# Other waiting times in the list scheduler that orders a transformer block's instructions

## The reference

```
x = x + layernorm(attention(layernorm(x)))
x = x + layernorm(ffn(layernorm(x)))
attention: qkv = x @ Wqkv.T + b;  16 query heads, 8 key heads of 128, in pairs
           p = softmax(q1 k1) - lam * softmax(q2 k2)   (causal)
           o = rmsnorm(p @ v) * w;  out = o @ out_w.T + b
ffn:       Hadamard transform, silu(gate) * up (1024 wide), Hadamard, down
```

## Time and profile before

| | |
|---|---|
| median of 3 runs | 1295.7 us (1291.06 to 1301.3) |
| profiled execution | 1293.1 us, span 1291.3 us |
| PE busy | 1168.3 us, 90% |
| DVE busy | 1064.9 us, 82% |
| ACT busy | 1025.2 us, 79% |
| POOL busy | 852.8 us, 66% |
| mean granted TensorE clock | 0.987 |

### The profile page before, as it was taken

How to read it: one execution, slowest core, us unless ns; L and a number is a source line. 1 busy time by engine, 2 the same in 40 slices (tenths; PEclk the granted TensorE clock), 3 DMA queues, 4 the chain that set the end, 5 groups by cost and what they waited for, 6 DMA issues and landing times.

```text
span 1291.3 us, 26698 instructions
## 1 busy us (share of the span) xinstructions
PE 1168.3 (90%) x8110; PEld 829.5 (64%) x8110; DVE 1064.9 (82%) x2723; ACT 1025.2 (79%) x2596; POOL 852.8 (66%) x1208
## 2 busy tenths in 40 slices
PE   6888999889899989899899898999888888889998
PEld 4556766566676666566666666567665565677887
DVE  5888999898979998988889988888788998946545
ACT  4778898798878889898889889897878888856341
POOL 3387777665676676666667776656659896776532
PEclk8999999999999999999999999999999999999999
DMA  3054545554355445444554555534564454640001
GB/s 127 26 106 81 99 87 86 86 102 82 48 121 96 88 85 93 97 76 76 103 97 81 95 84 86 102 68 90 103 97 87 75 106 88 101 93 1 29 17 37
DMA packets 368156, 106.64 MB, mean 83 GB/s; under 512 B 359312, under 2 KB 365712, under 8 KB 367504
## 3 DMA queue, kind: packets, MB, share of 16 engines
q1 hardware_dynamic: 366672, 103.37, 43.8%
q10 hardware_dynamic: 1344, 1.57, 0.4%
HBM read 14.71 MB, written 2.10 MB: 13 GB/s over the span
## 4 chain that ended last, share of the span: by engine, by line
PE 44%; DVE 30%; issue 8%; POOL 6%; ACT 6%; DMA 5%; SPq 2%; ACTq 0%; DVEq 0%; POOLq 0%
DVE p L1473 7%; DVE mx L1459 6%; PE score_bank L1187 6%; PE score_bank L1052 5%; PE score_bank L1058 4%; PE score_bank L1055 4%; DVE score_bank L1454 3%; ACT e_all L1227 3%; DVE negmx L1466 3%; POOL e_all L1748 2%; DMA oT<-o 2%; PE turn_bank L1080 2%; PE turn_bank L1082 2%; PE turn_bank L1081 2%; DMA p16T<-p 2%
## 5 line engine op out<-in xcount | busy, mean ns | idle before, releaser
L1227 ACT ACTIVATE e_all<-score_bank,negmx,few 128x512 f32<-128x512 f32 (+2 forms) x576 | 413.1, 727 | 64.1 <-DVE negmx L1466 50.9
L1748 POOL TENSOR_TENSOR e_all<-e_all 128x512 f32<-128x512 f32 (+3 forms) x320 | 367.8, 1164 | 36.4 <-ACT e_all L1242 24.1
L1052 PE MATMUL score_bank<-k,q 128*128 128x512 f16 (+2 forms) x640 | 223.8, 350 | 53.5 <-issue 24.9
L1459 DVE TENSOR_REDUCE mx<-score_bank 128x1 f32<-128x512 f32 (+1 forms) x384 | 241.4, 636 | 28.0 <-PE score_bank L1058 27.1
L1473 DVE SCALAR_TENSOR_TENSOR p<-e_all,gain,p 128x512 f16<-128x512 f32 (+3 forms) x320 | 248.1, 791 | 6.6 <-ACT p L1249 6.1
L1055 PE MATMUL score_bank<-k,q 128*128 128x512 f16 (+2 forms) x640 | 223.0, 348 | 0.3 <-DVE k L1534 0.3
L1058 PE MATMUL score_bank<-k,q 128*128 128x512 f16 (+2 forms) x640 | 223.0, 348 | 0.0
L1249 ACT ACTIVATE p<-e_all,gain 128x512 f16<-128x512 f32 (+3 forms) x320 | 203.1, 665 | 22.2 <-POOL e_all L1748 21.8
L1799 POOL TENSOR_SCALAR ratio<-s,inv,neg_lam 128x1 f32<-128x1 f32 x128 | 57.1, 446 | 168.4 <-DVE inv L1736 168.0
L1052 PEld LDWEIGHTS score_bank<-k,q 128*128 128x128 f16 x640 | 62.2, 97 | 138.0 <-issue 60.2
L1080 PE MATMUL turn_bank<-v,p16T 128*128 128x256 f16 x512 | 140.5, 274 | 9.4 <-DMA p16T<-p 9.3
(11 more groups left out here) (377 smaller groups left out, 2779.0 us busy)
## 6 DMA issues: line engine op xcount, KB each, us to landing
p16T<-p SPq DMA_TRANSPOSE x320, 3.1
w_raw<-in_w_qkv_dram SPq DMA_DIRECT2D x3, 1024.0 KB, 5.7
w_raw<-in_w_o_dram SPq DMA_DIRECT2D x4, 512.0 KB, 3.4
oT<-o SPq DMA_TRANSPOSE x128, 2.5
bv<-in_hidden_dram SPq DMA_DIRECT2D x8, 256.0 KB, 2.9
w_raw<-in_w_ug_dram SPq DMA_DIRECT2D x4, 512.0 KB, 3.5
out_dram<-e SPq DMA_DIRECT2D x16, 128.0 KB, 1.7
e<-in_w_d_dram SPq DMA_DIRECT2D x1, 1024.0 KB, 6.8
```

What stands on the lines that cost most here:

```text
L1052: pe.matmul(bank[:, 0:w], qh, kh, start=True, stop=False)
L1227: act.activation(e, S[k % NS][:, 0:w], ACT.Exp, bias=negmx[:, d % 2, m, s:s + 1], scale=-1.0 if alone else unit[:, g], accum_out=ssum[:, d ...
L1459: dve.tensor_reduce(mx[:, d % 2, m, s, c:c + 1], S[k % NS][:, 0:w], X, ALU.max)\
L1748: pool.tensor_tensor(a, a, b, ALU.add).then_inc(p_pool, 1)
```

## The change

Only numbers and bookkeeping of `plan()` are changed. No instruction is added, removed or altered; the order in which the engines issue them may become another one, and with it the semaphore values and which step uses which of the four work banks.

- The lag after PE goes from 0.12 to 0.2, after ACT from 0.17 to 0.145, after DVE from 0.14 to 0.12, after POOL from 0.1 to 0.135.
- What PE waits for from another engine is seen by it a further 0.1 later (`LOAD_LAG`, through a second set, `seen_by_pe`). PE's own steps count as seen by PE at once.
- The lag of a transpose behind its issue goes from 2.2 to 2.9 (`TURN_LAG`).
- `SWITCH_US` would lengthen a score step that follows another kind of step; it is 0.0.

```diff
-LAG = {"ACT": 0.17, "DVE": 0.14, "POOL": 0.1, "SP": 0.0}
+LAG = {"PE": 0.2, "ACT": 0.145, "DVE": 0.12, "POOL": 0.135, "SP": 0.0}
+LOAD_LAG, SWITCH_US, TURN_LAG = 0.1, 0.0, 2.9
...
-                        add("T", "SP", "SPLIT", (d, jj), 0.3 + 0.002 * ww, [("DVE", "SPLIT", (d, jj))] + room, 0, 2.2)
+                        add("T", "SP", "SPLIT", (d, jj), 0.3 + 0.002 * ww, [("DVE", "SPLIT", (d, jj))] + room, 0, TURN_LAG)
...
-                add("X", "SP", "OX", o, 1.2, [("DVE", "OL", o)] + ([("PE", "OP", o - 4)] if o >= 4 else []), 0, 2.2)
+                add("X", "SP", "OX", o, 1.2, [("DVE", "OL", o)] + ([("PE", "OP", o - 4)] if o >= 4 else []), 0, TURN_LAG)
...
-        if any(x not in done for x in needs(kind, what)):
+        if any(x not in seen_by_pe for x in needs(kind, what)):
...
-            if last is not None and (*evicted[last[0]].split(), last[1]) not in done:
+            if last is not None and (*evicted[last[0]].split(), last[1]) not in seen_by_pe:
...
-                us = pe_us(kind, what)
+                us = pe_us(kind, what) + (SWITCH_US if kind == "S" and ran[-1] in ("PV", "OP") else 0)
+                ran.append(kind)
...
-                ending.append((now[0] + us + 0.12, count[0], ("PE", kind, what)))
+                ending.append((now[0] + us + LAG["PE"], count[0], ("PE", kind, what)))
+                seen_by_pe.add(("PE", kind, what))
...
         ending.append((now[0] + us + op.lag + LAG[engine], count[0], (engine, op.kind, op.what)))
+        ending.append((now[0] + us + op.lag + LAG[engine] + LOAD_LAG, count[0], ("to PE", (engine, op.kind, op.what))))
...
+        seen_by_pe.update(name[1] for at, _, name in ending if at <= now[0] + 1e-9 and name and name[0] == "to PE")
```

More of the change, by code:

```diff
@@ L179, in plan @@
     _, pt_blockers = ring(widths, PT_ROOM)
-    steps, orders, done = [], {e: [] for e in ("ACT", "DVE", "POOL", "SP")}, set()
+    steps, orders, done, seen_by_pe = [], {e: [] for e in ("ACT", "DVE", "POOL", "SP")}, set(), set()
     waiting, ending, now, count = {}, [], [0.0], [0]
+    ran = ["X"]
     scaling, mixed = set(), set()
```

## The result

The changed kernel takes 1305.62 us (median of 7 runs, 1303.2 to 1307.47) against 1295.04 us before (7 runs, 1291.06 to 1301.3): ratio 1.008, 95% interval 1.0054 to 1.0105. It is slower by 0.8%, where 1281 us and a gain were forecast, and just outside the range (1304). The profiled execution took 1303.2 us with a span of 1301.4, so the comparison of the two spans, 10.1 us apart, stands for the comparison of the medians, 10.6.

The account below looks back on a forecast made before the run. PE was taken as the bound, DVE close behind. Ceilings 31.2 (transposes) + 10.7 (scores) = 41.9 us, of which about 13 was taken: 1293.1 - 13 = 1280, plus 2.6 for the median gives 1282.7; forecast 1281, range 1266 to 1304.

Parts of the forecast that it names:

- the tail: From 1160 us on, written out by hand: claimed to keep its order and last as long as before.
- a ceiling of 31.2: PE's 40 waits for transposes, 37.0 us: a turn longer by 0.78 gives back at most 40 x 0.78 = 31.2 us.
- to about 20: Expected sign: PE's 37.0 us of waits for transposes fall most, to about 20, and ACT's 12.6 with them.
- The worst stretch: Attention stretch from 900 to 1100 us, with 172.0 us of PE work in 200: claimed to come up.
- the sum: Total over the attention stretches: ceiling 31.2 + 10.7 = 41.9 us, of which about 13 us was taken as gain.
- score waits fall by up to 10.7 us: PE's 79 waits before score chunks, 47.1 us: handoffs planned 0.135 longer give back at most 10.7 us.
- The ceiling of 41.9: Most that PE's idle time could give back: 31.2 from waits for transposes plus 10.7 from score waits.
- the middle of 13: Gain taken, about 13 us: the middle between nothing and 25 us, five stretches at the best one's level.
- the best stretch: Attention stretch from 300 to 500 us: 187.2 us of PE work in 200, against a mean of 182.2.
- The slow rival: Products held back by the overlong turn, SP and ACT waiting in 19 places: 15 us slower, 1311; chance 0.17.
- Nothing that can be measured: Rival: the order changes but everything ends up waiting for DVE; 1293 to 1296, give or take 6; chance 0.25.
- the estimate of 2.6 us: Skill's rule for a transpose transfer, 2.0 + 0.6 us: the old plan's 3.52 ample, the turn's term nothing or a loss.

Follow-up runs that it names:

- b_noise3: Kernel before (old lags), every planned duration except PE's multiplied by a random factor 0.98 to 1.02 (seed 3), old order of WK and LN 2 on DVE: 1301.81 us.
- turn 2.21: Kernel before with only the turn's lag (a transpose's lag behind its issue) at 2.21 in place of 2.2: 1289.76 us, ratio 0.9968.

## Why the prediction was wrong

**What held.** PE stayed the bound with DVE close behind. Nothing changed in the tail: 132 us from 1160 on hold 125.65 us of PE work before, and 132 us from 1170 on hold 125.98 after. The longer turn did shorten the waits for transposes, by 22.3 us out of a ceiling of 31.2, which is more than the forecast's "to about 20", and ACT's with them. The worst stretch did come up, from 172.0 to 174.8.

**The step that failed is the sum.** It took idle time removed from PE in one place as time won, and let score waits fall by up to 10.7 us; they rose by 27.9. The ceiling of 41.9 added two classes of waits as if each shrank by itself, and the middle of 13 rested on the best stretch as a level that better lags would bring everywhere. The measured value of that term is -0.9 us (89.1 to 90.0 idle). The closing condition of the prediction (transfer waits fall, score waits rise as much, idle stays near 89) is what came.

**What was missing.** Two terms. The clock: I took PE's busy time as fixed, the same within a few us, and it rose by 8.2 us with the stretches at the lower clock, which is most of the 10.1 between the two spans. A sum of waits had no place for the length of the single wait. And the draw: I never asked what a random order with unchanged costs would give. That is 6.9 us above the kernel before, half as much as the whole gain of 13 that I forecast, and would have left about half of that gain at the centre.

**The rivals.** The slow rival had the right sign but the wrong place: products aren't held back behind a full ring. SP's waits for PE, which it wanted above 24.8 us, are

```profile
SPq L951 <- PE turn_bank L1088: 29.1, 8, 7.0
...
SPq L951 <- PE proj_bank L1088: 0.9, 2, 0.7
```

30.0 us in 10 places, 5 more, while ACT's fell to 8.5. It priced 15 us on them. Its other sign, transposed probabilities that PE reads long after they landed, is absent: matched in the order of issue, PE reads the 320 transposes 3.4 us after landing in the median, against 4.4 before. "Nothing that can be measured" was 1293 to 1296 give or take 6, and missed too. The Trainium skill's rule on the fixed cost of a transfer (DMA: Bandwidth & Descriptors, "Anatomy of one DMA") spoke against a longer turn. The page fits that rule to transfers issued by GpSimd, and these are issued by SP; the estimate of 2.6 us lies under the measured median of 3.1. The time agrees with the direction, but not by this mechanism, since the waits for transposes did shorten.

**What makes the score waits longer** is settled only for single places. The longest, 3.38 us, in the timeline of the changed kernel:

```profile
1001.06 0.16 DVE L1472 TENSOR_TENSOR negmx<-few 128x1 f32<-128x1 f32 x1
...
1001.37 1.26 POOL L1894 TENSOR_TENSOR v_sum<-w_raw 128x512 f32<-128x512 f32 x1
...
1002.72 0.63 ACT L1362 ACTIVATE wkv_hi<-v_sum 128x512 fp32r<-128x512 f32 x1 [1.70 <-POOL v_sum L1894]
...
1003.26 0.76 ACT L1233 ACTIVATE e_all<-score_bank,negmx,few 128x512 f32<-128x512 f32 x1
...
1004.21 0.32 PE L1058 MATMUL score_bank<-k,q 128*128 128x384 f16 x1 [3.38 <-issue]
```

The exponential's bias is ready at 1001.22. ACT has a piece of the feed-forward weights ahead of it in its order, which waits 1.70 us for a fold on POOL; the exponential starts at 1003.26 and PE's next score at 1004.21. That the plan took this filler to fit there is argued from the order and not shown. ACT's wait for the bias rose in sum from 48.6 us (between 60 and 1160) to 66.4, yet a redraw with the old lags has 64.7 (b_noise3), so that number doesn't carry the cause. Why longer lags make fewer and longer waits of the same idle time stays open.

## What to carry to other kernels

A list scheduler's output is a draw: before crediting a better cost model, redraw the order a few times with unchanged mean costs and compare against that spread (here 1289.8 to 1304.6 us around a kernel at 1294), since the order in hand may sit at the lucky end of it, as here. Shortening one class of waits of the bounding engine is a gain only if the sum of its idle time falls; read that sum, its busy time at the granted clock, and how many of its waits are long, ahead of the class. The best order found, turn 2.21, beats both kernels by 0.3% and 1.2% and is itself only a draw.

## What the runs showed of the hardware

Two handoff values fit the one place of the trace from which they were read (0.14 from the end of an exponential to PE's load, 0.19 from the last score matmul's columns to DVE), and yet the plans with them were no faster. Low-clock stretches stand right behind waits of PE of 2.20 us (ended at 397.17) and 3.38 us (ended at 1004.21), though not behind long waits alone, and not behind each: after one of 2.59 us that ended at 733.29 the clock stayed up. Where they stand, a wait costs more than its length. At the front a delay of DVE by one group of statistics, 1.39 + 0.38 us, let PE go on 1.1 us later (25.74 against 24.61) and became 2.4 us at the first score chunk (32.1 against 29.7), because the matmuls between ran at the lower clock.
